# Sandwich transformer on one core: local attention in blocks of 32 queries and 64 keys, inverse norms by two Newton steps, projections up to two tiles ahead

## The reference, cut to what matters

```python
q, k, v = split(x @ Wqkv)                 # 16 heads of 64
q = q / max(norm(q), 1e-12) * qs;  k = k / max(norm(k), 1e-12) * ksc
q = q * cos * scale + rotate_half(q) * sin * scale     # k with 1/scale
# windows of w = 32: a query sees its own window and the one before,
# and of these only keys j with i-32 <= j <= i
attn = softmax(where(mask, -big, 8 * q @ k.T));  out = attn @ v
x = x + out @ Wo
```

## Time and profile before

| | us |
|---|---|
| median of 3 runs | 2024.64 (2019.8 to 2025.11) |
| the profiled execution, its own time | 2023.72 |
| its span, first to last instruction | 2021.9 |
| busy in the span: PE, PEld | 1896.6, 1437.1 |
| busy: POOL, ACT, DVE | 1669.2, 1593.2, 1555.0 |
| mean granted PE clock | 0.985 of full speed |

### The profile page before, as it was taken

The page is one execution under the profiler, slowest core; times in us unless marked ns, Lnnn a source line. Parts: engine busy times, 40 slices in busy tenths (PEclk is TensorE's granted clock), DMA queues, the critical chain, the costliest instruction groups (busy, mean ns, idle before and its releaser), DMA issues.

```text
span 2021.9 us, 67246 instructions
## 1 busy us (share of the span) xinstructions
PE 1896.6 (94%) x22192; PEld 1437.1 (71%) x22192; DVE 1555.0 (77%) x4021; ACT 1593.2 (79%) x5612; POOL 1669.2 (83%) x1264
## 2 busy tenths in 40 slices
PE   7997999989999989999988999998999999999997
PEld 5665777765777765777764777774777775777773
DVE  5786888867888866888866888866888876888876
ACT  6775888876888875888875888885888885888883
POOL 3326999986999986999985999985999995999971
PEclk9997999999999999999999999999999999999999
DMA  3002111112111112211112112212211111111110
GB/s 122 14 11 66 48 47 47 47 43 77 48 47 47 47 43 76 51 47 47 47 43 63 49 47 55 52 34 73 49 47 47 47 48 38 49 47 47 47 46 21
DMA packets 44547, 99.42 MB, mean 49 GB/s; under 512 B 7345, under 2 KB 24209, under 8 KB 43505
## 3 DMA queue, kind: packets, MB, share of 16 engines
q1 hardware_dynamic: 44400, 97.59, 18.5%
HBM read 19.59 MB, written 1.05 MB: 10 GB/s over the span
## 4 chain that ended last, share of the span: by engine, by line
PE 80%; ACT 8%; issue 6%; DVE 3%; POOL 2%; DMA 0%; DVEq 0%; ACTq 0%; SPq 0%; POOLq 0%
PE bank L1198 10%; PE bank L1211 9%; PE bank L1246 8%; PE bank L1225 8%; PE bank L1191 8%; PE bank L1227 6%; PE bank L1232 6%; PE bank L1226 6%; PE bank L1182 3%; ACT kT L548 3%; PE bank L1328 3%; ACT prob L510 2%; PE bank L1317 2%; PE bank L1315 2%; PE bank L1238 2%
## 5 line engine op out<-in xcount | busy, mean ns | idle before, releaser
L345 POOL TENSOR_TENSOR rn<-n2c,half_neg 128x8 f32<-128x8 f32 x384 | 636.7, 1658 | 93.2 <-DVE n2c L837 92.5
L510 ACT ACTIVATE prob<-bank,nmax 128x96 f32<-128x96 f32 x1536 | 501.2, 350 | 133.7 <-DVE nmax L787 133.4
L347 POOL TENSOR_TENSOR tsum<-tc_,ts_ 128x512 f32<-128x512 f32 x384 | 489.6, 1275 | 0.0
L350 POOL TENSOR_TENSOR w_nat<-tsum,rn 128x512 f32<-128x512 f32 x384 | 400.5, 1043 | 37.7 <-POOL tsum L347 15.1
L830 DVE TENSOR_REDUCE n<-nat 128x8 f32<-128x512 f32 x384 | 262.6, 684 | 150.4 <-ACT nat L526 139.8
L510 ACT ACTIVATION_READ_ACCUMULATOR prob<-bank,nmax 128x1 f32 x1536 | 331.5, 216 | 7.0 <-issue 7.0
L787 DVE TENSOR_REDUCE nmax<-bank 128x4 f32<-128x384 f32 x384 | 196.3, 553 | 152.7 <-PE bank L1191 152.7
L1198 PE MATMUL bank<-idf,prob 128*96 128x128 f32 x1536 | 245.6, 283 | 46.9 <-ACT kT L548 30.1
L519 ACT ACTIVATE pT<-bank 96x512 f32<-96x512 f32 x384 | 230.4, 600 | 74.6 <-PE bank L1198 72.6
L840 DVE TENSOR_TENSOR ts_<-bank,ropeL 128x256 f32<-128x256 f32 x768 | 286.2, 414 | 0.0
L1225 PE MATMUL bank<-w_hi,xs 128*128 128x512 f32 x576 | 277.5, 482 | 3.7 <-DVE xs_lo L819 2.3
(11 more groups left out here) (125 smaller groups left out, 3311.2 us busy)
## 6 DMA issues: line engine op xcount, KB each, us to landing
vspace<-v_nat SPq DMA_DIRECT2D x96, 384.0 KB, 4.0
vspace<-v_nat SPq DMA_DIRECT2D x96, 256.0 KB, 3.4
vspace<-v_nat SPq DMA_DIRECT2D x95, 128.0 KB, 2.3
nat<-w_qkv SPq DMA_DIRECT2D x5, 1536.0 KB, 8.6
wo<-w_o SPq DMA_DIRECT2D x6, 512.0 KB, 4.0
w<-w SPq DMA_DIRECT2D x6, 341.0 KB, 3.1
shared<-w_qkv SPq DMA_DIRECT2D x1, 1536.0 KB, 11.1
w<-w SPq DMA_DIRECT2D x6, 192.0 KB, 3.1
```

Of the source, the lines that this page charges most:

```text
L345: nc.gpsimd.tensor_tensor(rn[:, r, :], n2c[:, r, :], half_neg[:, 0:8], ALU.pow).then_inc(pool_step, 1)
L347: nc.gpsimd.tensor_tensor(tsum[:, r, :], tc_[:, r, :], ts_[:, r, :], ALU.add).then_inc(pool_step, 1)
L350: nc.gpsimd.tensor_tensor(w_nat[:, r, :].rearrange("p (h d) -> p h d", d=D), tsum[:, r, :].rearrange("p (h d) -> p h d", d=D), rn[:, r, :] ...
L510: last = nc.scalar.activation(prob[:, 4 * b + i, :], SB[b][:, i * SPAN:(i + 1) * SPAN], ACT.Exp, bias=nmax[:, p, 8 * G + 4 * b + i:8 * G + ...
```

## The change

Attention of the layers in four windows of 32 queries with their 64 keys: the mask has 64 columns, the scores of a group take 32 matmuls instead of 16 (32 queries by 64 keys over 64 rows: eight positions), the probabilities of two heads fill 128 columns and are transposed together (8 transposes and 2 copies per tile in place of 16 and 4), and the values are weighed by 32 matmuls per group instead of 16 (64 rows deep, 32 queries by 64 channels, eight positions), into two banks, of which one (YB) also holds the output projection. `vw` holds for each window its 64 keys, for the even heads in the upper and the odd heads in the lower 64 partitions; ten DMAs per tile fill it. The inverse norm of two blocks is taken together, from a seed that ACT makes out of the exponent bits (`seed`), by two Newton steps of four POOL operations each (`refine`); the first tile of each layer keeps the power. The projections 0 and 1 (and square and rotary of them) of tile t+2 are done within tile t, those of the second tile of a layer ahead of its first tile. The first attention (heads of 8 channels) stays as it is.

```diff
+PJ, SB, YB = bank[0:2], bank[2:4], bank[7]
+OB, O2 = bank[5], (bank[5][:, 0:HB // 2], bank[7][:, P:P + HB // 2])
...
-        eng.dma_start(vw[WIN:SPAN, p, 0, :], v_nat[0:HALF, p, :]).then_inc(v_seen[p], 16)
-        eng.dma_start(vw[:, p, 1, :], v_nat[WIN:P, p, :]).then_inc(v_seen[p], 16)
+        for b in range(2):
+            eng.dma_start(vw[b * SEEN + WIN:(b + 1) * SEEN, p, 0, :].rearrange("p (g c) -> p g c", g=2),
+                          four_heads(p, b, 0, WIN)).then_inc(v_seen[p], 16)
+        for w in range(1, BLOCKS):
+            for b in range(2):
+                eng.dma_start(vw[b * SEEN:(b + 1) * SEEN, p, w, :].rearrange("p (g c) -> p g c", g=2),
+                              four_heads(p, b, (w - 1) * WIN, SEEN)).then_inc(v_seen[p], 16)
         if not last:
             at_least(eng, pv_done, t * 2)
-            eng.dma_start(vw[0:WIN, 1 - p, 0, :], v_nat[P - WIN:P, p, :]).then_inc(v_prev[1 - p], 16)
+            for b in range(2):
+                eng.dma_start(vw[b * SEEN:b * SEEN + WIN, 1 - p, 0, :].rearrange("p (g c) -> p g c", g=2),
+                              four_heads(p, b, P - WIN, WIN)).then_inc(v_prev[1 - p], 16)
...
+    def rotary_sum(t, j):
+        Q, r = t * 4 + j, j % 2
+        at_least(eng, w_ready, Q - 1)
+        eng.wait_ge(pj_dve, Q + 1)
+        nc.gpsimd.tensor_tensor(tsum[:, r, :], tc_[:, r, :], ts_[:, r, :], ALU.add).then_inc(sum_ready, 1)
+    def refine(t, g, seeds):
+        s2, K = n2c[:, :, :].rearrange("p r h -> p (r h)"), (t * 2 + g) * 8
+        eng.wait_ge(seeded, seeds)
+        nc.gpsimd.tensor_tensor(rn_a[:, :], s2, rn0[:, g, :], ALU.mult).then_inc(refined, 1)
+        eng.wait_ge(refined, K + 1)
+        nc.gpsimd.tensor_tensor(rn_b[:, :], rn_a[:, :], rn0[:, g, :], ALU.mult).then_inc(refined, 1)
+        eng.wait_ge(refined, K + 2)
+        nc.gpsimd.tensor_tensor(rn_c[:, :], step_c[:, 0, :], rn_b[:, :], ALU.subtract).then_inc(refined, 1)
...
+        nc.gpsimd.tensor_tensor(rn_b[:, :], rn_a[:, :], rn_z[:, :], ALU.mult).then_inc(refined, 1)
+        eng.wait_ge(refined, K + 6)
+        nc.gpsimd.tensor_tensor(rn_c[:, :], step_c[:, 1, :], rn_b[:, :], ALU.subtract).then_inc(refined, 1)
+        eng.wait_ge(refined, K + 7)
+        at_least(eng, w_ready, t * 4 + 2 * g)
+        nc.gpsimd.tensor_tensor(rn[:, :], rn_c[:, :], rn_z[:, :], ALU.mult).then_inc(refined, 1)
...
+    def rotated(t, j, first=False):
+        Q, r, g = t * 4 + j, j % 2, j // 2
+        eng.wait_ge(sum_ready, Q + 1)
+        eng.wait_ge(refined, (t * 2 + g) * 8 + (4 * r + 4 if first else 8))
+        at_least(eng, tp_full, Q - 1)
+        nc.gpsimd.tensor_tensor(
+            w_nat[:, r, :].rearrange("p (h d) -> p h d", d=D), tsum[:, r, :].rearrange("p (h d) -> p h d", d=D),
+            rn[:, r * 8:r * 8 + 8].rearrange("p (h o) -> p h o", o=1).to_broadcast([P, 8, D]), ALU.mult).then_inc(w_ready, 1)
+    def rotate(t, seeds):
+        rotary_sum(t, 0)
+        rotary_sum(t, 1)
+        refine(t, 0, seeds)
+        rotated(t, 0)
+        rotary_sum(t, 2)
+        rotated(t, 1)
+        rotary_sum(t, 3)
+        refine(t, 1, seeds + 1)
+        rotated(t, 2)
+        rotated(t, 3)
...
         eng.wait_ge(max_ready, t * 4 + (2 * G + b + 1))
-        at_least(eng, pt_full, t * 4 + (2 * G + b - 1))
+        at_least(eng, pt_full, t * 2 + G)
         for i in range(4):
-            head = 8 * G + 2 * i + b
+            h = 2 * i + b
+            slot = 2 * (h % 4) + h // 4
             last = nc.scalar.activation(
-                prob[:, 4 * b + i, :], SB[b][:, i * SPAN:(i + 1) * SPAN], ACT.Exp,
-                bias=nmax[:, p, 8 * G + 4 * b + i:8 * G + 4 * b + i + 1], accum_out=lsum[:, p, head:head + 1])
+                probs[:, slot * SEEN:(slot + 1) * SEEN], SB[b][:, i * SEEN:(i + 1) * SEEN], ACT.Exp,
+                bias=nmax[:, p, 8 * G + 4 * b + i:8 * G + 4 * b + i + 1],
+                accum_out=lsum[:, p, 8 * G + h:8 * G + h + 1])
         last.then_inc(p_ready, 1)
...
+    def probs_out(t, G, at):
+        eng.wait_ge(pt_full, t * 2 + (G + 1))
+        at_least(eng, pv_done, t * 2 + (G - 1))
+        nc.scalar.activation(pT[:, 4 * G:4 * G + 4, :], RING[at][:, :].rearrange("p (h q) -> p h q", h=4),
                              ACT.Copy).then_inc(pt_evac, 1)
...
+    def seed(t, g):
+        eng.wait_ge(n2c_ready, t * 4 + (2 * g + 2))
+        at_least(eng, refined, (t * 2 + g) * 8 - 8)
+        nc.scalar.activation(rn0[:, g, :], n2c[:, :, :].rearrange("p r h -> p (r h)").bitcast(mybir.dt.int32), ACT.Exp,
+                             scale=LOG_SCALE, bias=log_bias[:, 0:1]).then_inc(seeded, 1)
...
         heads3 = "p (h d) -> p h d"
         nc.vector.tensor_reduce(n2[:, r, :, 0], sq[:, r, :].rearrange(heads3, d=D), AX.X, ALU.add
                                 ).then_inc(n2_ready, 1)
         k = 2 * (j % 2)
+        at_least(eng, sum_ready, Q - 1)
         nc.vector.tensor_tensor(
...
-        nc.vector.tensor_reduce(n2c[:, r, :], n2[:, r, :, :], AX.X, ALU.max).then_inc(n2c_ready, 1)
         for a in range(2):
             lo, hi = a * (D // 2), (1 - a) * (D // 2)
             last = nc.vector.tensor_tensor(
                 ropeL[:, k + 1, n, lo:lo + D // 2].rearrange("p (o d) -> p o d", o=1
                                                              ).to_broadcast([P, 8, D // 2]), ALU.mult)
         last.then_inc(pj_dve, 1)
+        eng.wait_ge(n2_ready, Q + 1)
...
         at_least(eng, p_ready, t * 4 + 2 * G)
         for b in range(2):
-            nc.tensor.matmul(SB[b][:, 0:4 * SPAN], idb[:, :].bitcast(bf16),
-                             msk[:, n, :].bitcast(bf16).rearrange("p (o k) -> p o k", o=1).to_broadcast([P, 4, SPAN]),
+            nc.tensor.matmul(SB[b][:, 0:4 * SEEN], idb[:, :].bitcast(bf16),
+                             mskB[:, n, :].bitcast(bf16).rearrange("p (o k) -> p o k", o=1).to_broadcast([P, 4, SEEN]),
                              start=True, stop=False, skip_group_check=True)
         for i in range(4):
-            g, cols = 4 * G + i, slice(i * SPAN, (i + 1) * SPAN)
-            for half in range(2):
-                qs, ks = slice(half * HALF, (half + 1) * HALF), slice(half * HALF, half * HALF + SPAN)
+            g, cols = 4 * G + i, slice(i * SEEN, (i + 1) * SEEN)
+            for w in range(BLOCKS):
+                qs, ks = slice(w * WIN, (w + 1) * WIN), slice(w * WIN, w * WIN + SEEN)
                 for b in range(2):
                     rows = slice(b * D, (b + 1) * D)
                     last = nc.tensor.matmul(SB[b][qs, cols], qT[rows, p, g, qs], kT[rows, p, g, ks],
                                             start=False, stop=True, skip_group_check=True)
...
-    def transpose_probs(t, G, b, at):
-        eng.wait_ge(p_ready, t * 4 + (2 * G + b + 1))
+    def transpose_probs(t, G, at):
+        eng.wait_ge(p_ready, t * 4 + (2 * G + 2))
         for i in range(4):
-            last = nc.tensor.transpose(RING[at][0:SPAN, i * P:(i + 1) * P], prob[:, 4 * b + i, :], idf[:, :])
+            last = nc.tensor.transpose(RING[at][:, i * P:(i + 1) * P], probs[:, 2 * i * SEEN:2 * (i + 1) * SEEN],
+                                       idf[:, :])
         last.then_inc(pt_full, 1)
...
+        eng.wait_ge(pt_evac, t * 2 + (G + 1))
         at_least(eng, o_evac, t * 2 + G)
-        eng.wait_ge(v_seen[p], seen(t, p))
-        at_least(eng, v_prev[p], prev_in(t, p))
+        if G == 0:
+            at_least(eng, y_free, t)
+        eng.wait_ge(v_seen[p], seen_block(t, p))
+        at_least(eng, v_prev[p], prev_block(t, p))
+        eng.sem_inc(pv_begun, 1)
         for i in range(4):
-            for b in range(2):
-                head, a = 8 * G + 2 * i + b, (2 * i + b) * D
-                for half in range(2):
-                    qs = slice(half * HALF, (half + 1) * HALF)
-                    last = nc.tensor.matmul(OB[qs, a:a + D], pT[:, 4 * b + i, qs],
-                                            vw[:, p, half, head * D:(head + 1) * D], start=True, stop=True,
+            for w in range(BLOCKS):
+                qs = slice(w * WIN, (w + 1) * WIN)
+                for b in range(2):
+                    rows = slice(b * SEEN, (b + 1) * SEEN)
+                    last = nc.tensor.matmul(O2[b][qs, i * D:(i + 1) * D], pT[rows, 4 * G + i, qs],
+                                            vw[rows, p, w, (4 * G + i) * D:(4 * G + i + 1) * D], start=True, stop=True,
                                             skip_group_check=True)
         last.then_inc(pv_done, 1)
```

More of the change, by code:

```diff
@@ L601, in start @@
                     values(t0, 0, 1)
+                if part == 5:
+                    copy_input(2, 0)
+                    square(t0 + 1, 0)
+                    square(t0 + 1, 1)
             def layer(l, last):
@@ L701, in layer @@
                     start(t0 + TILES, 4)
-            for part in range(5):
+                    start(t0 + TILES, 5)
+            for part in range(6):
                 start(0, part)
@@ L979, in tile @@
```

(25 more changed lines are left out.)

305 lines of the change are left out of this document (168 added, 137 removed).

## The result

The changed kernel takes 2013.28 us (median of 4 runs, 2009.81 to 2015.42), the kernel before 2024.88 us on the same chip (4 runs, 2019.8 to 2028.26): a ratio of 0.9943, 95% interval 0.9917 to 0.997. It is faster, as forecast, but by 12 us and not by 121; 1903 was wrong, and the result lies above the range.

What follows compares the result with a forecast made beforehand. POOL and PE were taken as walls at 16.04 and 15.8 us a tile; a tile falling from 16.2 to 14.8, 84 times, saves 118 us, closing tiles 3, so 2023.7 becomes 1903 us; range 1850 to 1990.

Steps and rivals of the forecast that it cites:

- A Newton step was put at 0.30: POOL: 16 small steps a tile at 0.30 us, 4.8 us, replace four powers, leaving POOL at 14.4 us.
- the fill's 0.11: POOL: a 16-column fill takes 0.11 us, the nearest small row; with its price POOL would stand at 12.4 us.
- A burst was put at 0.75: PE: each burst of 64 score or weighing records takes 0.75 us, between ends of 0.61 and 1.64.
- The wait foreseen for the residual: PE queue: the weighing's new wait for `residual` holds up PE by at most some tenths of a microsecond.
- PE's 14.5: PE per tile: 15.8 less 0.88, 0.24, 0.14 and 0.66, plus 0.6 of added waits, makes 14.5 us.
- DVE's 13.2: DVE per tile: smaller maxima, about -0.13 each, and four products for two, +0.27, give 13.2 us, below the walls.
- The floor of 25.6 ns a record: Rival, PE bursts: a record every 25.6 ns however small; PE 17.4 us a tile, 2125 us in all; chance 0.12.
- A burst of 1.0: Rival, PE bursts: record supply binds in part; burst 1.0, PE 15.5, tile 15.8 us, 1987 in all; chance 0.18.
- a Newton step of 0.41: Rival, POOL: steps cost 0.41 or more, 6.5 us like the powers; POOL stays the wall, about 2020 us; chance 0.03.
- So four lengths lie between 14.1 and 14.5: Tile: POOL 14.4, PE 14.5 and two cross-tile loops, 14.1 and about 14, nearly coincide; 0.3 added gives 14.8 us.
- the loop through POOL and DVE's clamp: Across tiles: block 3's sum, Newton steps, products, sums, Newton steps, then DVE's clamp, head product and rotary 3: about 14 us.
- the opening tile ... taken as even, with 3 us gained in the closing tiles: Layer ends: opening keeps the powers, two projections move to the layer before; taken as even, closing tiles gain 3 us.

Runs made afterwards that it cites:

- the changed one with its two other edits: Changed kernel with clamped sums copied per pair of blocks, closing tile's shifted copies before its exps, PE, ACT and DVE layers written out: 1946.28 us, ratio 0.9615.

## Why the prediction was wrong

Free of the jumps over layers, the old kernel (2003.4) and the changed one with its two other edits (1946.3) show what the change is worth and where it stops. The pieces in us, with the prediction's terms, and the changed kernel against the one before, both as they are:

```
                              old, no jumps   new, no jumps   diff.   predicted   as changed
84 steps after the opening       1357.6          1249.1       -109      -118         -82
6 openings                         95.4           115.2        +20         0          -1
6 closing tiles                   100.3           120.3        +20        -3         +29
5 times gate to next scores       219.0           228.5        +10         0         +37
```

The openings are the first of each layer's 15 steps. The profiled execution was to lose 121 us and lost 8: of the 113 between them, 36 are in the steps, 32 in the closing tiles, 37 between gate and scores, 9 in the first and last piece, and -1 in the openings.

**The prices of POOL, the bursts and ACT held.** A Newton step was put at 0.30 us and is 0.30; the fill's 0.11 was no price for it. POOL stands at 4 x (1.27 + 1.04) + 16 x 0.30 = 14.0 us a tile with its hand-overs, for 14.4; its busy time is 12.69, since the profile leaves hand-overs out. A burst was put at 0.75 and takes 0.79 to 0.83. ACT is busy 13.01 us for 13.2. The wait foreseen for the residual came to 5.1 us in the whole run. PE's 14.5 was 13.9 of work and 0.6 of added waits before bursts; it is busy 14.35, and those waits (weight loads of scores and weighing, "issue") grew from 82.7 to 92.7 us over 96 tiles, 0.1 a tile. So PE's sum came out by two errors that nearly cancel.

DVE's 13.2 was 0.85 too high. That is no wall, but 0.6 of it is in one instruction that the change leaves as it is, the copy of the previous keys (before, then after: count, busy us, mean ns):

```profile
L812 DVE TENSOR_SCALAR kT<-kT,follows 128x256 f32<-128x256 f32 x96 | 85.8, 894 | 0.0
L930 DVE TENSOR_SCALAR kT<-kT,follows 128x256 f32<-128x256 f32 x96 | 35.9, 374 | 0.0
```

Before, all 13 of these copies between 500 and 720 us start while POOL is in a product of 1.04 us (L350), end some 0.15 us behind that product's end, and take 0.93 to 0.96 us; in the kernel with the powers back, copies with no POOL operation beside them take 0.34 to 0.36. In the changed kernel POOL's operations beside the copy take 0.22 us, and the copy takes 0.35. The DVE operation stretched with the POOL operation beside it, and Newton steps in place of long operations shortened DVE's work too.

**The rivals by their condition.** The floor of 25.6 ns a record fell: 64 records in 0.83 us are 13 ns each, and 10 ns from first to last. The prediction read 25.6 as the time from record to record, but it has the end of the burst in it: on the timeline of before the last of the 32 score records starts 0.65 us after the first, 21 ns apart, so that the trace did not agree with the rule that it was said to agree with. The rule of the Trainium skill that start to start never drops below about 25 ns (TensorE: Matmul & The Clock Gate, section "Wait — 56ns, not 53.3ns?") does not hold here for records in separate positions of the array. A burst of 1.0 and a Newton step of 0.41 did not come either. No rival named what did happen.

**The first step that failed: "So four lengths lie between 14.1 and 14.5", with 0.3 for all.** The four stood side by side, and the loop through POOL and DVE's clamp ("the sum of block 3, Newton steps (2.4), two products, ... about 14 us") was one of them. They are tied together. The chain of waits of the changed kernel, from POOL's sum of block 3 to the same sum two tiles on (start, us, what):

```profile
832.68 0.54 POOL tsum L394
...
844.34 0.17 DVE n2c L962
...
845.00 0.42 DVE o_nat L914
...
845.56 0.63 PE bank L1371 x4
...
854.11 0.39 PE bank L1308 x2
...
860.73 0.67 ACT nat L622
...
862.63 0.76 DVE ts_ L954 x2
...
863.46 0.54 POOL tsum L394
```

POOL's sums, Newton steps and products last until the clamp may start (11.7 us); behind the clamp stands the product of heads, behind that PE's output transpose, and then PE's queue up to the scores of the next tile (854.11); from there it goes on through ACT's exponentials and the square of block 3 (860.73), and DVE's rotary step, back to POOL. That is 30.8 us for two tiles, 15.3 to 15.4 each, where each loop alone was put at 14. The prediction had the clamp and the product of heads in its loop, as work of DVE on the way to the rotary step, and asked what is queued behind the weighing's wait; it did not ask what on PE waits behind the clamp's. The loop's own sum was wrong as well: the terms as listed make about 13.1 us, not 14, and DVE's part, put at 2 us, takes 3.4 (874.95 to 878.31 on its timeline), so that "about 14" is near by luck. With the clamp free of the Newton steps, a step falls from 15.28 to 14.94, and the 84 steps by 26 us of the 36. What sets the 14.9 was not taken apart, so that its nearness to the forecast 14.8 does not show the sum of prices right.

**The second: "the opening tile ... taken as even, with 3 us gained in the closing tiles".** This cost 66 us at closing tiles and between layers, in three parts. The jump back of PE's program, which lay beside queued matmuls in the kernel before (2.5 us in all), stands bare in the changed one: 3 x 7.4 = 22 us; the prediction did not look at loops at all. The two copies in ACT's queue: 17 us. The rest, 26 of the 66, is near what stays in these two pieces between the jump-free kernels (20 + 10), and is not settled further. Two more projections ahead of each layer are in it, and moving them later made the kernel slower. The granted clock is in it too, a term that the prediction put at nothing without a reason: in these two pieces TensorE is at the lower level for 51 us in the new jump-free kernel and for none in the old one, and at half the clock that can cost up to 26 us. Whether the stops of PE bring the low clock or the clock only lengthens them, no run took apart.

That the openings rose by 20 us between the jump-free kernels and by nothing between the others is no contradiction: in the old kernel 15 us of jumps stood in them, and in the changed one they are 17.9 us, not 19.3, where the other engines could run ahead during PE's 7.4 us.

What makes an opening tile 19.3 us where the old one takes 15.5 is POOL's work, by the timelines. In both it is POOL that fills the opening, 17.05 of 19.3 us and 15.11 of 15.5 (windows above). In the new kernel, POOL begins the power of the opening tile's own fourth block only at 763.23, after the first mask at 762.7, and is done with that block at 767.4; then come the four blocks of the second tile, up to 782.07, with the next first mask at 782.0:

```profile
763.23 1.69 POOL L443 TENSOR_TENSOR rn<-n2c,half_neg 128x8 f32<-128x8 f32 x1
...
780.03 2.04 POOL L421 TENSOR_TENSOR w_nat<-tsum,rn 128x512 f32<-128x512 f32 x2
```

In the old one the fourth block is done at 784.64, with the first mask at 784.2, and the opening holds the second tile's blocks alone. The opening was not "even": it has one block of powers more, 4.2 us.

**Why so little came of 82 us.** Of the 82 us that the steps gained, the layer ends took back 66. A faster step brought 1 us, 84 times; the six ends of layers lost 5 to 16 us each.

## What to carry to other kernels

Where a change fills the pipeline further across iterations, price its ends from the trace of before as carefully as its middle: which queue holds what the first work after the loop needs, and what covers a jump. For every buffer that a shortened or lengthened step reads, ask who waits to overwrite it and what stands behind that wait in its queue; a second copy of 16 numbers a partition was worth 24 to 32 us here. Compare the granted clock of the ends too, before and after. For small matmuls in separate positions of the array, see that neighbours in the queue go around the positions: here the other order made the kernel slower than the old one.

## What the runs showed of the hardware

A jump back over these layers costs PE 7.3 to 7.4 us, ACT 3.1 to 3.7 and DVE 2.1 to 2.8 when nothing queued covers it, and removing one engine's jump exposes the next engine's. In the kernel before, whose openings showed it only as tiles of 20 to 22 us instead of 15.5, it was worth 21 us, more than the whole change brought. Matmul records with 64 rows by 32 columns of weights start 10 ns apart in eight positions, 19 ns in two. A POOL operation on 16 columns takes 0.22 us, and 0.08 more until one that needs it starts. A DVE copy of 128x256 fp32 takes 0.35 us alone and 0.95 when a POOL product of 1.04 us is under way beside it.
